# Second attention with its scores in the lower rows of the array, beside projected values and similarities in the upper rows, masks first

## What is computed

```python
q = (x @ Wq).reshape(b, n, HEADS, DIM) * DIM ** (-0.5)
kv_scores, indices = _pk(x, Wq_pk, pk_keys)          # 16 of 4096 entries for each position and head
k = jnp.einsum('bnhk,bnhkd->bnhd', kv_scores, keys_table[ind])
v = jnp.einsum('bnhk,bnhkd->bnhd', kv_scores, values_table[ind])
sim = jnp.einsum('bihd,bjhd->bhij', q, k)
sim = jnp.where(causal, sim, neg)
attn = jax.nn.softmax(sim, axis=-1)
out = jnp.einsum('bhij,bjhd->bhid', attn, v)
...
return out @ Wo
```

## Time and profile before

| what | value |
|---|---|
| median of 3 executions | 1962.24 us (1961.16 to 1962.26) |
| the profiled execution | 1959.13 us |
| its span, first to last instruction | 1957.3 us |
| TensorE busy, mean granted clock | 97%, 0.991 |
| VectorE, ScalarE, GpSimd busy | 82%, 75%, 67% |
| one item in the steady loop | about 26.7 us |

### The profile page before, as it was taken

How to read it: one execution, slowest core, us unless ns; L and a number is a source line. 1 busy time by engine, 2 the same in 40 slices (tenths; PEclk the granted TensorE clock), 3 DMA queues, 4 the chain that set the end, 5 groups by cost and what they waited for, 6 DMA issues and landing times.

```text
span 1957.3 us, 43650 instructions
## 1 busy us (share of the span) xinstructions
PE 1898.5 (97%) x11464; PEld 1470.7 (75%) x11464; DVE 1607.9 (82%) x4824; ACT 1466.0 (75%) x2969; POOL 1313.8 (67%) x1575
## 2 busy tenths in 40 slices
PE   5997899999999999999999999999999999999997
PEld 3765577777777777777777777777777777777776
DVE  3646788888888888888888888888888888888886
ACT  3763477887877787877877777777877777877775
POOL 1112377777777777777777777777777777777775
PEclk9998999999999999999999999999999999999999
DMA  3001100001000200020000100020001100020001
GB/s 108 2 1 47 57 22 20 20 20 61 14 20 20 64 18 16 17 64 20 20 20 16 57 20 20 20 62 16 17 20 38 47 19 16 14 64 20 20 18 28
DMA packets 118094, 58.00 MB, mean 30 GB/s; under 512 B 109696, under 2 KB 116032, under 8 KB 116733
## 3 DMA queue, kind: packets, MB, share of 16 engines
q1 hardware_dynamic: 115250, 56.75, 11.1%
q10 hardware_dynamic: 2795, 0.70, 0.2%
HBM read 24.55 MB, written 0.70 MB: 13 GB/s over the span
## 4 chain that ended last, share of the span: by engine, by line
PE 76%; issue 7%; POOL 6%; DVE 1%; ACT 0%; POOLq 0%; DMA 0%; SPq 0%; DVEq 0%; ACTq 0%
PE ps L978 26%; PE ps L986 14%; PE ps L969 13%; PE ps L990 7%; PE ps L1028 4%; POOL k_W_low L1374 3%; PE ps L1046 3%; PE ps L963 2%; PE ps L1038 2%; PE ps L1013 2%; PE ps L1000 1%; PE ps L1006 1%; POOL k_aS L1316 0%; PE ps L1029 0%; POOL k_cand L1330 0%
## 5 line engine op out<-in xcount | busy, mean ns | idle before, releaser
L1540 DVE SCALAR_TENSOR_TENSOR k_W<-ps,k_W 128x688 f32<-128x688 f32 x1028 | 892.6, 868 | 230.5 <-ACT k_W L1184 211.1
L1374 POOL TENSOR_TENSOR k_W_low<-k_W,k_W_high 128x688 fp32r<-128x688 f32 x513 | 850.5, 1658 | 337.9 <-ACT k_W_high L1189 337.9
L1184 ACT ACTIVATE k_W<-ps 128x688 f32<-128x688 f32 x1029 | 765.7, 744 | 364.0 <-PE ps L969 354.1
L978 PE MATMUL ps<-k_W,k_tab 128*128 128x344 f32 x2048 | 676.5, 453 | 0.0
L969 PE MATMUL ps<-k_X,sel 128*128 128x344 f16 x2058 | 471.3, 310 | 8.1 <-DVE k_W L1540 7.4
L978 PEld LDWEIGHTS ps<-k_W,k_tab 128*128 128x128 f32 x2048 | 366.1, 190 | 127.5 <-issue 0.5
L1189 ACT ACTIVATE k_W_high<-k_W 128x688 fp32r<-128x688 f32 x513 | 395.6, 771 | 0.0
L986 PE MATMUL ps<-k_W_high,k_tab_high 128*128 128x344 f32 x1024 | 385.6, 379 | 0.0
L986 PE MATMUL ps<-k_W_high,k_tab_low 128*128 128x344 f32 x1024 | 324.6, 320 | 0.0
L969 PEld LDWEIGHTS ps<-k_X,sel 128*128 128x128 f16 x2058 | 176.3, 99 | 177.9 <-issue 79.1
L990 PE MATMUL ps<-k_W_low,k_tab_high 128*128 128x344 f32 x1024 | 244.3, 319 | 0.0
(11 more groups left out here) (233 smaller groups left out, 2313.0 us busy)
## 6 DMA issues: line engine op xcount, KB each, us to landing
k_tab<-in_tables SPq DMA_DIRECT2D x9, 2048.0 KB, 7.3
k_X<-k_spl SPq DMA_TRANSPOSE x390, 2.4
k_xs<-x2T SPq DMA_DIRECT2D x33, 172.0 KB, 2.2
k_qT<-k_qs SPq DMA_DIRECT2D x33, 86.0 KB, 2.0
cst<-in_consts SPq DMA_DIRECT2D x1, 1024.0 KB, 20.6
wts<-in_weights SPq DMA_DIRECT2D x1, 896.0 KB, 12.9
cst<-in_consts SPq DMA_DIRECT2D x1, 874.5 KB, 17.3
xr<-in_xrows SPq DMA_DIRECT2D x1, 750.0 KB
```

What stands on the lines that cost most here:

```text
L978: mm = mm_(sums, tab[:, slot, at + k, :], W[:, d % RING, k, :], start=(d == 0 and k == 0), stop=(d == NDC - 1 and k == 1))
L1184: A(W[:, d % RING, :, :], ps[:, 2 * (d % 2):2 * (d % 2) + 2, 0:LOUT], ACT.Exp).then_inc(e_done, 1)
L1374: G.tensor_tensor(W_low[:, q % SPLIT_RING, :, :], W[:, d % RING, :, :], W_high[:, q % SPLIT_RING, :, :].bitcast(F32), ALU.subtract).then_i ...
L1540: V.scalar_tensor_tensor(W[:, d % RING, :, :], ps[:, 2 * (d % 2):2 * (d % 2) + 2, 0:LOUT], 0.0, W[:, d % RING, :, :], ALU.is_ge, ALU.mult) ...
```

## The change

The three pieces `project_values`, `similarities` and `attention_scores` become one piece at step 7. First come the three masks, now as wide as the scores (`causb` is 384 columns: 256 zeros, then the triangle). Then the scores read only partitions 64 to 127 (the lower row half of the array), the projected values and the similarities only partitions 0 to 63 (the upper half), in an order in which a matmul of one half stands beside one of the other. `xs` becomes two tiles of 64 partitions, one for each sequence of the pair, loaded by two DMAs. The values go to unused columns of banks 6 and 7; since one of them shares bank 7 with the last scores, TensorE waits for it (`last_mm`) before these. ScalarE copies the values at step 9 ahead of the probabilities, after the row maxima, and the similarities at step 8; VectorE takes `halves_max` at step 9; SyncE issues the transposes ahead of the reload of `xs`. The wait for the copied values (`vw_ready`) moves to `turn_probabilities`.

```diff
+                def project_values(t, head):
+                    t0, m = TT[t]
+                    bank, c0 = value_area(t)
+                    rhs = wos[0:64, head, :] if isinstance(head, int) else wos[0:64, bass.ds(head, 1), :].rearrange("p a d -> p (a d)")
+                    return mm_(ps[0:m, bank, c0:c0 + 64], kv[0:64, t0:t0 + m], rhs, start=(bank == MID0), stop=(bank == MID0))
+
+                def causal_mask(t, pj):
+                    t0, m = TT[t]
+                    bank, c0 = score_area(t, pj)
+                    mm_(ps[0:m, bank, c0:c0 + t0 + m], eyeb[0:m, 0:m], causb[0:m, 256 - t0:256 + m], start=(t != 1), stop=False)
+
+                def key_scores(t, pj):
+                    t0, m = TT[t]
+                    bank, c0 = score_area(t, pj)
+                    return mm_(ps[0:m, bank, c0:c0 + t0 + m], qT[64:128, pj, t0:t0 + m], kv[64:128, 0:t0 + m], start=False, stop=(t > 0))
+
+                def similarities(t, par, head):
+                    t0, m = TT[t]
+                    return mm_(ps[0:m, MID0, 128 * t:128 * t + 128], xs[:, par, t0:t0 + m],
+                               wf[0:64, 0, bass.ds(head, 1), :, :].rearrange("p a b k -> p (a b) k"), start=True, stop=True)
...
-                    wait_alone(pe, vw_ready, i + 1)
...
+                    if following is not None:
+                        pe.wait_ge(sim_ready, i + 2)
+                        wait_alone(pe, xs_ready, pairs * 32 + 32)
+                    wait_alone(pe, kv_ready, i + 1)
+                    for t in range(NT):
+                        causal_mask(t, pj)
+                    key_scores(0, pj)
+                    project_values(2, head).then_inc(last_mm, 1)
+                    key_scores(1, pj)
+                    project_values(0, head)
+                    project_values(1, head).then_inc(vw_mm, 1)
+                    pe.wait_ge(last_mm, i + 1)
+                    key_scores(2, pj).then_inc(s_mm, 1)
+                    if following is not None:
+                        for t in range(NT):
+                            mm = similarities(t, *following)
+                        mm.then_inc(sim_mm, 1)
...
+                    pe.wait_ge(vw_ready, i + 1)
...
-                                project_values(i, g // 4 if par else ((g + 31) // 4) % 8)
-                            if d == 6:
-                                similarities(i + 2, par, (g + 1) // 4, g)
                             if d == 7:
-                                attention_scores(i, nj, g)
+                                attention_scores(i, nj, g, g // 4 if par else ((g + 31) // 4) % 8, (par, (g + 1) // 4))
...
+                    act.wait_ge(nmax_done, i * 3 + 3)
+                    A(vw[:, 0:2, :], ps[:, MID0, NT * 128:NT * 128 + 128], ACT.Copy)
+                    A(vw[0:88, 2, :], ps[0:88, MID1, LOUT:LOUT + 64], ACT.Copy).then_inc(vw_ready, 1)
...
-                                copy_projected_values(i)
-                            if d == 7:
+                            if d == 8:
                                 copy_similarities(i + 2)
                             if d == 9:
+                                copy_projected_values(i)
                                 for t in range(NT):
                                     probabilities(i, nj, t)
...
-                            if d == 8:
+                            if d == 9:
                                 halves_max(i + 2, False)
...
+                        turn_scores(i + 1, 1 - par)
                         if par == 1:
                             wait_alone(sync, sim_mm, i + 3)
-                            sync.dma_start(xs[:, :], x2T[:, bass.ds((pair + 2) % NPAIR, 1), :].rearrange("p a s -> p (a s)")).then_inc(xs_ready, 16)
-                        turn_scores(i + 1, 1 - par)
+                            for b in range(2):
+                                sync.dma_start(xs[:, b, :], x2T[64 * b:64 * b + 64, bass.ds((pair + 2) % NPAIR, 1), :].rearrange("p a s -> p (a s)")).then_inc(xs_ready, 16)
```

48 lines of the change are left out of this document (16 added, 32 removed).

## The result

The changed kernel takes 1949.05 us (median of 4, 1947.92 to 1950.18), the kernel before on the same chip 1961.91 us (median of 4): ratio 0.9935, 95% interval 0.9918 to 0.9952. So it is 12.9 us faster, where 25 us were forecast (1936.5 us). The profiled execution took 1947.92 us with a span of 1946.1 us, 11.2 us less than the span before.

What follows compares the result with a forecast made beforehand. TensorE's queue was taken to bound the kernel: 0.69 us saved less 0.30 us for ScalarE, over 64 items, plus 0.7 us behind the loop, gave 1933.4 us, set at 1936.5 for the median; range 1922 to 1950, 8 in 10 1914 to 1956.

Steps and rivals of the forecast that it cites:

- Sign and what bounds the kernel: Steady loop: a queue of TensorE work, busy 97% of the span, so work removed saves time; faster at 0.84.
- The 0.7 us forecast behind the loop: Behind the loop, values no longer precede the scores with a copy between, though a 0.3 us copy precedes the probabilities: 0.7 us less.
- The block of step 7: TensorE's merged block: masks 0.32, overlapping half-row streams 1.27 and borders 0.40 us, 1.99 us in all; odd item saves 0.68 us.
- The borders: Step 7: switching the array into half rows and back costs 0.20 us each, 0.40 us an item, bounds 0.1 to 0.5.
- The even item: Its masks and scores stop waiting for copied values but wait about 0.3 us for ScalarE's query copy; 0.71 us saved.
- ScalarE in steps 9 to 12: Value and similarity copies behind the log weights delay exponentials, then VectorE's weights and TensorE: 0.30 us an item, bounds 0 to 0.45.
- at nothing: VectorE's six maxima of the halves, moved behind the next weights, cost nothing; another 0.1 us if the cover is gone.
- rival A: ScalarE's delay does not reach TensorE, whose waits stay at 4 us: 1917 us, or 1908 with cheap borders; chance 0.15.
- Transposes: SyncE's transposed scores keep 0.16 us of slack, not binding, but capping an odd item's saving at 0.85 us; reload behind them free.
- C: Step 7: streams of unequal length run one after the other, block 3.16 us, slower by 50 us: 2012 us; chance 0.06.
- D: Step 7: waiting for the last value matmul before the last score matmul holds the upper half, up to 0.2 us: 1949 us; within forecast's 0.62.
- B: Step 7: the halves keep program order by passes, streams 1.60 us in place of 1.27, total 1958 us; chance 0.13.

Runs made afterwards that it cites:

- run 6: The kernel before, with only its three projected-value matmuls reading 64 rows, alone between full-array neighbours; 1981.36 us, ratio 1.0100.
- run 1: The changed kernel with TensorE's wait for ScalarE's query copy checked last ahead of the masks, behind semaphores long satisfied; 1934.08 us, ratio 0.9867.
- run 10: The kernel of run 9 with ScalarE's third probabilities and last value tile copy behind the exponential of step 10; 1947.22 us, ratio 0.9925.
- Run 2: The changed kernel with ScalarE's copies of the similarities and two of three value tiles moved to the start of step 8; 1936.24 us, ratio 0.9872.
- run 5: The changed kernel with SyncE's reload of xs ahead of the transposes again, as before the change; 2032.32 us, ratio 1.0358.
- run 7: The kernel of run 3 with ScalarE's query copy ahead of the high part of the next item's scores in step 6; 1921.99 us, ratio 0.9795.
- run 8: The changed kernel with score matmuls reading all 128 partitions, so values and similarities cannot run beside them; 2064.77 us (one execution).
- run 4: The changed kernel with all three value matmuls ahead of all score matmuls in the program; 1956.5 us, ratio 0.9977.
- run 9: The kernel of run 3 with ScalarE's query copy and scores' high part ahead of the weights' high part at step 6, both items; 1947.51 us, ratio 0.9926.
- run 3: The changed kernel with both the query-copy wait put last and ScalarE's step 8 copies made early; 1920.31 us, ratio 0.9795.
- run 12: The kernel of run 9 with VectorE's three comparisons of the chosen scores one step later in odd items; 1922.95 us, ratio 0.9793.

## Why the sign was right and the size half of it

**Sign and what bounds the kernel: right.** What left TensorE's queue left the time; the distances between its log weights account for the span. The 0.7 us forecast behind the loop did not come: that part takes 18.79 us in place of 18.73.

**The block of step 7: right, 0.1 us too long.** Forecast 1.99 us, measured 1.89 us (odd) and 1.97 us (even). The borders were 0.40 us in the sum, from the earlier trace rows; run 6 gives 0.30 us for the pair, and the streams then keep the forecast 1.27 us. The odd item saved 0.70 us for 0.68 forecast.

**The even item: the step that failed.** It was put as "A wait of about 0.3 us takes the place of the one removed". The releaser was named rightly, and the copy was as late as forecast: it ended at 1038.40, 0.22 us behind the end of the low part at 1037.86 + 0.32, forecast 0.25. But the masks began about 0.8 us late, and the item saved 0.18 us in place of 0.71. Of the 0.5 us of excess, 0.46 us is the order of the waits (run 1), a cost that the prediction did not have at all: it took a semaphore long reached for free, and asked only when the last one comes, not what the sequencer still has to do after it. The 0.53 us in each even item are 17 us over 32 of them, more than the 13 by which the medians miss the forecast; the odd items and the term of ScalarE came out 2 us better than forecast.

**ScalarE in steps 9 to 12: the size right, the place half right.** Forecast 0.30 us, measured 0.28 us. But 0.16 us of it lie in step 10, and the rows put them on VectorE: the maxima, moved behind the weights and held by the similarity copy (`[0.34 <-ACT k_sS L1190]`), stand ahead of the next weights. The prediction had these "at nothing", with 0.1 us as the price if the cover is gone. In step 11 (0.12 us) the exponential behind the probabilities is late as forecast: 4.49 us after the log weights at 1013.84, where it was 3.95 us in the earlier trace rows (1023.80 against 1019.85), 0.54 us, forecast 0.66. But VectorE's queue, which the moved maxima lengthened, is as late as that: in run 10 the weights follow the start of the reciprocal ahead of them by 0.10 us with the exponential long done, and the change has this reciprocal at 1019.01 and the weights at 1019.14. So either would have held this step nearly as long, and that the sum came out at 0.28 is largely luck. Run 2 gives most of it back, but moves both causes at once; the 0.04 to 0.07 us that stay in step 11 are VectorE's queue (run 10). What the forecast said would show it, 20 us of waits of TensorE for VectorE, did not appear, because the loss hides in the tails of the matmuls. By its own test rival A would have been called true; distances between starts show that it is not.

**Transposes: right.** They bound nothing in the change, the reload behind them costs nothing, ahead of them it costs 83 us (run 5), and the cap showed as soon as the rest was faster (run 7).

**The rivals.** A falls (0.28 us an item are lost, though part of it by VectorE's queue and not by ScalarE). C falls: run 8 shows what one stream after the other costs, 3.75 us (forecast for C 3.16; run 8 has two borders' pairs more). D, the wait for the last value, has no row in the waits and the block is shorter than forecast, so it cost nothing that can be seen. B holds in a weak form: in the change the first similarity pass starts at 1013.03, 0.10 us before a score pass (1013.13) that stands ahead of it in the program, so the order is not strict, and the block of 1.89 us leaves no room for the 0.33 us that B wanted. In run 4 the order does cost 0.16 us. The rule of the Trainium skill ("TensorE: Matmul & The Clock Gate", Part 3: Packing small matmuls), matmuls start and end strictly in the order of the program, does not hold here for starts between the two row halves.

**The numbers.** Forecast saved 0.69 - 0.30 = 0.39 us an item; measured 0.44 - 0.28 = 0.16 us. The even item accounts for all of the miss (0.53 us in every second item). Run 1, which takes away what had been overlooked, lands at 1934 us, close to the forecast of 1936.5. That does not confirm each of the forecast's terms: step 7 of even items stays 0.4 us longer than that of odd items (3.61 and 3.19), where 0.3 was forecast, the borders are cheaper, and the 0.28 us in steps 10 to 12 have in part another cause.

## What to carry to other kernels

Put the wait that comes last behind all others: every wait written after it is paid for again, 0.09 to 0.15 us each here, on the path. When a step is moved off TensorE's queue, ask of the small steps on the other engines not only whether they have idle time, but what stands behind them in their own queue. A loss on TensorE that is shorter than a matmul's tail is in no list of waits; measure distances between starts. A wait can cost more than its length: in run 5, eight of 32 waits of 2.3 us were followed by a fall of TensorE's clock, 1.6 us each.

## What the runs showed of the hardware that was not expected

Semaphore checks that are already met take time one after the other on TensorE: five of them 0.46 us (run 1: from the end of the copy to the masks 0.60 us, reordered 0.14 us), 0.09 to 0.15 us from one to the next in the change's trace.

A way from whole to half rows of the array and back costs 0.30 us (run 6, 19.5 us over 64), against an estimated 1.26 us that running the halves side by side brings in this block (run 8's 1.86 us less two such ways).

Behind waits of 2.3 us on TensorE the granted clock fell to half for 3.4 us, eight times in 32 such waits (run 5); the change, whose waits from 300 to 1900 us are 0.7 us at most but for three of up to 1.5, has no such fall there.

VectorE's comparison of 100 fp32 columns, SBUF to SBUF, takes 257 ns when GpSimd pauses, and up to 1677 ns when GpSimd works; three of them took 4.11 us beside three GpSimd instructions without a gap (run 9), and each long one ends 0.07 us behind the end of a GpSimd instruction. A pause of 0.25 us (run 3) or a later place in VectorE's queue (run 12) takes it off the path. The Trainium skill ("SBUF — State Buffer", Who interferes with whom) says that VectorE's `tensor_scalar`, which the comparison is, can enter a mode in which it needs the pair of ports that it shares with GpSimd, and that whoever issues first has this pair for the whole instruction while the other fully blocks. The ends of the comparisons, at 1015.65 and 1006.85 against 1015.58 and 1006.78 of GpSimd's instructions, agree.
